# Stacked score operands laid out four partitions apart in a fused attention and convolution kernel

## The reference

```python
x = x + attention(group_norm(x))          # 32 groups
x = x + masked_conv3x3(group_norm(x))     # 256 -> 256 channels
# attention, its low half ("local scores" in this kernel): 4 heads of 32
q = (tokens @ l_q_w).reshape(B, H * W, 4, 32)             # 1024 tokens
kv = (pooled @ l_kv_w).reshape(B, 256, 2, 4, 32)          # 2x2 mean-pooled: 256 keys
attn = softmax(einsum('bnhd,bmhd->bhnm', q, k) * 32 ** -0.5)
lo = einsum('bhnm,bmhd->bnhd', attn, v) @ l_proj_w + l_proj_b
```

## Time and profile before

| | us |
|---|---|
| median of 3 runs | 351.7 |
| lowest, highest | 351.23, 353.86 |
| the profiled execution | 350.24 |
| its span in the profile | 348.0 |

### The profile page before, as it was taken

The page is one execution under the profiler, slowest core; times in us unless marked ns, Lnnn a source line. Parts: engine busy times, 40 slices in busy tenths (PEclk is TensorE's granted clock), DMA queues, the critical chain, the costliest instruction groups (busy, mean ns, idle before and its releaser), DMA issues.

```text
span 348.0 us, 4160 instructions
## 1 busy us (share of the span) xinstructions
PE 312.7 (90%) x1566; PEld 224.1 (64%) x1566; DVE 271.2 (78%) x489; ACT 148.7 (43%) x189; POOL 83.5 (24%) x46
## 2 busy tenths in 40 slices
PE   1996648999979899999799999999799999999995
PEld 1575334367866663788577745888488727877884
DVE  4953999679997696989979867789777847897572
ACT  2551628672582743553047854351255423031300
POOL 2026384540455020004900200008600200202000
PEclk9998958999989999999899999999899999999999
DMA  8789230009600000098011100296001000101002
GB/s 276 274 111 157 83 122 0 2 24 126 78 0 4 2 1 2 20 129 140 4 60 60 63 0 2 43 130 117 4 0 62 0 0 10 53 0 62 0 0 121
DMA packets 12067, 20.38 MB, mean 59 GB/s; under 512 B 2064, under 2 KB 8080, under 8 KB 11792
## 3 DMA queue, kind: packets, MB, share of 16 engines
q1 hardware_dynamic: 12048, 20.13, 28.3%
HBM read 7.93 MB, written 4.19 MB: 35 GB/s over the span
## 4 chain that ended last, share of the span: by engine, by line
PE 59%; DVE 26%; ACT 6%; issue 5%; DMA 3%; SPq 0%; DVEq 0%
PE slot L1136 29%; PE cps L1168 17%; DVE l_max L868 7%; PE slot L1212 7%; ACT probs L580 3%; PE cps L1212 2%; DMA ks<-probs 2%; DVE v_lo L834 1%; DVE mask L804 1%; PE cps L1136 1%; PE slot L1461 1%; DMA xy<-x 1%; DVE xy L909 1%; ACT p_w L628 1%; DVE xn L760 1%
## 5 line engine op out<-in xcount | busy, mean ns | idle before, releaser
L1168 PE MATMUL cps<-v_hi,cw_hi 128*128 128x512 f32 (+1 forms) x144 | 58.9, 409 | 3.6 <-DVE v_lo L834 2.9
L1168 PE MATMUL cps<-v_hi,cw_lo 128*128 128x512 f32 (+1 forms) x144 | 58.8, 409 | 0.0
L1168 PE MATMUL cps<-v_lo,cw_hi 128*128 128x512 f32 (+1 forms) x144 | 57.5, 399 | 0.0
L385 POOL TENSOR_TENSOR probs<-q_w,k_w 128x1024 f32<-128x1024 f32 x14 | 32.9, 2383 | 82.4 <-DVE rw L797 72.4
L868 DVE TENSOR_REDUCE l_max<-slot 128x4 f32<-128x1024 f32 x32 | 37.0, 1218 | 7.3 <-PE slot L1136 7.3
L580 ACT ACTIVATE probs<-slot 128x1024 f32<-128x1024 f32 x32 | 31.5, 1022 | 14.9 <-PE slot L1136 14.8
L1168 PEld LDWEIGHTS cps<-v_hi,cw_hi 128*128 128x128 f32 x144 | 28.1, 195 | 13.0 <-issue 5.3
L1168 PEld LDWEIGHTS cps<-v_hi,cw_lo 128*128 128x128 f32 x144 | 28.1, 195 | 7.7 <-issue 2.2
L1168 PEld LDWEIGHTS cps<-v_lo,cw_hi 128*128 128x128 f32 x144 | 28.1, 195 | 5.2
L368 POOL TENSOR_TENSOR mask<-rw 128x1024 f32<-128x1024 f32 x8 | 15.2, 1912 | 56.6 <-DVE rw L797 56.6
L1136 PE MATMUL slot<-xn_hi,w_hi 128*128 128x512 f32 (+1 forms) x68 | 27.2, 400 | 0.3 <-DVE xn_lo L726 0.3
(11 more groups left out here) (197 smaller groups left out, 633.5 us busy)
## 6 DMA issues: line engine op xcount, KB each, us to landing
xy<-x SPq DMA_DIRECT2D x8, 512.0 KB, 3.9
out<-xy SPq DMA_DIRECT2D x8, 512.0 KB, 2.6
qs<-probs SPq DMA_DIRECT2D x12, 256.0 KB, 5.8
qs<-probs SPq DMA_DIRECT2D x24, 128.0 KB, 8.2
raw_cw<-conv_w SPq DMA_DIRECT2D x2, 1152.0 KB, 6.8
ks<-probs SPq DMA_DIRECT2D x12, 128.0 KB, 6.9
probs<-h_qkv SPq DMA_DIRECT2D x2, 192.0 KB, 3.8
probs<-l_kv SPq DMA_DIRECT2D x2, 128.0 KB, 3.7
```

Source lines behind the costliest of these rows:

```text
L385: nc.gpsimd.tensor_tensor(product(b, j).rearrange("p (n w) -> p n w", n=NW), q_w[:].rearrange("p (n w) -> p n w", n=NW), k_w[:, j * G:(j + ...
L1168: ins = nc.tensor.matmul(cps[:, pos % 2, y0 * WT:y1 * WT], (cw_hi, cw_hi, cw_lo)[part][:, k, pos, dy + 1, o * P:(o + 1) * P], (v_hi, v_lo, ...
```

## The change

The three parts are no longer side by side. Part p of channel d goes to partition 4d + p, so each stacking DMA writes 32 partitions, four apart, over all 128. The fourth rows (4d + 3) take what stood in 96 and 97: the parts of the maxima go to partitions 3 and 7 (`SHIFT`). Both matmuls now contract over all 128 rows. For that, all of `ks` is set to 1.0 and all of `qs` to 0.0 by GpSimd at the start, where only two rows of `ks` were set. Since the block scores of the next image must not see the old maxima, SP zeroes partitions 3 and 7 of `qs` before each later image, with two DMAs of 16 KB from the zero columns of `l_max` (rows of 256 bytes), after a wait for all exponentials of the image before (`st_exp`); TensorE's wait on `stacked` counts them. For image 0, SP waits for the memsets (`ones`).

```diff
@@
-SC = 3 * HD
-SM = SC + 2
+PARTS = P // HD
+SHIFT = (PARTS - 1, 2 * PARTS - 1)
@@ stack(b), on SP
                 def queries(part, parts, n, done):
-                    sp.dma_start(qs[HD * part:HD * (part + 1), :, n].bitcast(F32),
+                    sp.dma_start(qs[bass.ds(part, HD, step=PARTS), :, n].bitcast(F32),
                                  parts[:, n].bitcast(F32)).then_inc(done, 16)
 
                 def keys(part, parts):
-                    sp.dma_start(ks[HD * part:HD * (part + 1)].bitcast(F32), parts.bitcast(F32)).then_inc(stacked, 16)
-
+                    sp.dma_start(ks[bass.ds(part, HD, step=PARTS)].bitcast(F32),
+                                 parts.bitcast(F32)).then_inc(stacked, 16)
+
+                if b == 0:
+                    sp.wait_ge(ones, 1)
+                else:
+                    sp.wait_ge(st_exp, b * LT)
+                    for i, row in enumerate(SHIFT):
+                        sp.dma_start(qs[row:row + 1].bitcast(F32),
+                                     l_max[i * 64:(i + 1) * 64, NB * HEADS:NB * HEADS + 64]).then_inc(stacked, 16)
                 sp.wait_ge(lq_act, b + 1)
@@ stack_maxima(b), on SP
-                    sp.dma_start(qs[SC + i:SC + i + 1].bitcast(F32), t.bitcast(F32)).then_inc(max_stacked, 16)
+                    sp.dma_start(qs[SHIFT[i]:SHIFT[i] + 1].bitcast(F32), t.bitcast(F32)).then_inc(max_stacked, 16)
@@
-        STACK, STACK_LATE, MAX_STACK = 6 * 16, 3 * 16, 2 * 16
+        STACK, SHIFTS, STACK_LATE, MAX_STACK = 6 * 16, 2 * 16, 3 * 16, 2 * 16
@@ GpSimd, at the start
-            nc.gpsimd.memset(ks[SC:SM].bitcast(F32), 1.0).then_inc(ones, 1)
+            nc.gpsimd.memset(qs[:].bitcast(F32), 0.0)
+            nc.gpsimd.memset(ks[:].bitcast(F32), 1.0).then_inc(ones, 1)
@@ pooled_scores(b, i), on TensorE
-                    last = mm(slot[score_slot(b, i)][:, half], ks[0:SM, h, t * P:(t + 1) * P], qs[0:SM, h, halves(half)],
+                    last = mm(slot[score_slot(b, i)][:, half], ks[:, h, t * P:(t + 1) * P], qs[:, h, halves(half)],
@@ block_scores(b, n), on TensorE
-                    ins = mm(flat[block_slot(b, n)][:, h * G:(h + 1) * G], qs[0:SC, h, n * P:(n + 1) * P], ks[0:SC, h],
+                    ins = mm(flat[block_slot(b, n)][:, h * G:(h + 1) * G], qs[:, h, n * P:(n + 1) * P], ks[:, h],
@@ front(b, conv), on TensorE
-                        pe.wait_ge(stacked, (b + 1) * STACK)
+                        pe.wait_ge(stacked, (b + 1) * STACK + b * SHIFTS)
```

## The result

| | before | after |
|---|---|---|
| median | 351.59 us (4 runs) | 345.87 us (4 runs) |
| lowest, highest | 351.23, 353.86 | 345.54, 346.5 |
| the profiled execution | 350.24 | 345.54 |
| its span | 348.0 | 343.7 |

The account below looks back on a forecast made before the run. Bound: image 0's scores wait for slow stacking copies, a bandwidth backlog at 126 GB/s. Maxima 4.6 us sooner, all else 0: 350.24 − 4.6 = 345.6 profiled, 351.7 − 4.6 = 347.1 us median; range 345.8 to 350.2.

Parts of the forecast that it names:

- Step 1: Image 0's stacking copies: rate rises from 126 towards 370 GB/s, first scores at about 26.0, 3.3 us sooner.
- Step 2: VectorE's maxima of image 0: without a standstill they end at 36.3 instead of 40.85, 4.6 us sooner.
- Step 3: After image 0's maxima: these end last, so the softmax and all later stages shift by about 4.5 us.
- Step 4: GpSimd's memsets at the start: end at 5.8 to 9.0 us, cost nothing; without slack 1.4 us at most.
- the first bound: GpSimd's memsets at the start: time goes by elements in a row, 4.8 us for 4096 + 1024, ending at 5.8.
- Step 5: SP before each later image: its wait and zeroing DMAs, some 1.2 us, are hidden in a gap of over 15.
- Step 6: TensorE's score matmuls: contraction over 128 rows instead of 96 or 98 costs nothing, 0.40 us either way.
- Step 7: Block scores and maxima of later images: gain of 0 to 0.3 us, taken as 0.
- A: Stacking copies speed up little: 351.7 us at 126 GB/s, 349 at 160; chance 0.08 unchanged, 0.09 partial.
- D: Stacking copies four rows apart crowd fewer write ports, 63 GB/s, time near 385 us; chance 0.04.
- C: At the start, the memset holds up VectorE's first statistics, a slip of 1.6 us, time 348.7; chance 0.04.
- B: In other phases, moved VectorE and GpSimd meetings and clock falls hand back 1 to 2 us, 348.5 to 350; chance 0.07.

Follow-up runs that it names:

- the first control: The changed kernel again, unaltered, run beside the trials of turn order and early x: 346.48 us, ratio 0.9864 to the kernel before.
- the second: The changed kernel once more, unaltered, run beside the kernel with both groups of GpSimd's convolution weights held back: 346.05 us, ratio 0.9865 to the kernel before.
- the first trials: Old rows in the changed kernel (349.55 us), value_half(1) earlier in the kernel before (349.4), maxima turned before window scores in the changed kernel (349.08); kernel before beside them 350.51.
- the second set: The changed kernel with further copies appended after its last store, varying source rows, size and which 32 rows are written: 385.63 us, one run.
- the first trial: The changed kernel with GpSimd's outer convolution weights held until VectorE finishes image 0's window softmax: 346.86 us, ratio 0.9879 to the kernel before.

## Why the prediction was right, point by point

**Bound.** Right: the wait at the earlier trace rows was one for bandwidth. With the old rows alone it comes back whole. The 1.2 us to the first byte and the 0.8 us of completion in that sum stand in none of its rows.

**Step 1, the rate.** Right in kind and size: between 126 and 370 the upper end was taken, and 381 came out. The landing was over-estimated, without effect. The estimate was 2.3 to 2.6 us, and the DMA issues of the changed kernel show 2.1:

```profile
ks<-probs SPq DMA_DIRECT2D x12, 128.0 KB, 2.1
```

TensorE did not wait for the keys at all. The scores start at 25.71 and not 26.0 because TensorE starts them 0.23 us behind the start of the last value matmul (25.48), where the forecast counted from its end at 25.88. The argument that the destination alone sets these copies apart was too simple, since an HBM source writes the same rows at 228.

**Step 2, the maxima.** The term was 4.6 us and measured 5.2. End forecast 36.3, seen 35.62. The 0.7 between them: 0.3 from the earlier start of the scores, 0.1 because VectorE follows TensorE after 0.75 us and not 0.85, 0.2 because no gap is left, and 0.1 because the eight take 9.16. The granted clock was 1.00 from 20 to 34 us, as the step needed.

**Step 3, what follows.** This step failed. "So VectorE's maxima end last" left out one order: TensorE turns the maxima only after the window scores, and these need GpSimd's last product. The prediction had that product's end right (35.0; seen 34.99) but set it only against ScalarE's need. That end was itself an effect of the change: before, GpSimd waited 2.90 us for the second half of the values and ended at 37.86. Four matmuls more and the turning may start at 36.9, where the maxima alone would have had it at 35.8, and with it come `group_means` and the window softmax. Before, the maxima ended last at 40.85 and GpSimd's products, at 37.86, had 3 us to spare; now the products and the window scores behind them are the later ones. Of the 5.2 us, 1.1 are handed back here. The two errors, 0.6 too little in step 2 and 1.1 too much here, leave 4.1 us. The span is 0.2 us shorter elsewhere, and the time outside the span 0.4 us shorter (350.24 − 348.0 = 2.2, 345.54 − 343.7 = 1.8), which no step has. That makes 4.7: forecast 345.6 for the profiled execution, seen 345.54. So closely the sum came out by luck; its terms were further off. ScalarE's statistics, forecast to start at 31.7 and end at 36.1, start at 32.50 and end at 36.96; the run with x early shows that this costs nothing.

**Step 4, memsets.** Free, and the first bound was the right one:

```profile
0.99 3.52 POOL L447 MEMSET qs<- 128x4096 f32 x1
4.45 0.95 POOL L448 MEMSET ks<- 128x1024 f32 x1
```

3.52 us where 3.8 was forecast, the end at 5.4, and the next work at 7.65 against 7.64 before; 2.25 us of slack are left. Time goes by elements in a row: 0.95 us for 1024 whether 2 partitions or 128.

**Step 5, SP.** Right. The zeroing DMAs are issued at 55.74 and the queries behind them at 72.28, so 16 us pass between. For images 2 and 3 it is 17 and 20 us.

**Step 6, 128 rows of contraction.** Right, though it is 32 or 30 more rows and not "two to four":

```profile
L1145 PE MATMUL slot<-qs,ks x64: 388/396/775, 40.8 to 272.2; 128*128 128x512 f32 x64
```

**Step 7, later images.** Right at 0, and the sign of being wrong that it had, image 1 waiting on its copies, did not show: its first scores wait 0.62 us for ScalarE and not for a DMA.

```profile
84.44 1.22 PE L1145 MATMUL slot<-ks,qs 128*128 128x256 f32 x8 [0.62 <-ACT v_w L524]
```

Image 1 is instructive. Its maxima's parts reach SP at 102.45 instead of 107.45, 5.0 us sooner, while the image as a whole starts 4.2 sooner. But the next thing on its chain is GpSimd's products, 9.42 us from 95.69, and TensorE's last window scores behind them at 105.16. The 0.8 us extra are gone by the next image (141.94 against 146.16).

**From the profiled execution to the median.** The forecast took the offset of 1.5 us to hold for the changed kernel too. It was 0.33 there, which is 1.1 of the 1.2 us between 347.1 and 345.87. The granted clock of the stretch from 26 to 62 us differs between executions of one kernel. In the windows of the profiled executions of the changed kernel it was 0.97 from 26 to 44 us and 0.84 from 44 to 62 in the first, 0.92 and 0.79 in the first control, 0.96 and 0.85 in the second, and the spans were 343.7, 344.7 and 343.3. The larger scatter of the kernel before goes with the clock too: of the 25 executions beside the first trials the slowest, 353.8 us, has the lowest mean granted clock, 0.951, and the five under 349.7 us have 0.970 to 0.974. Which of the two causes the other no run shows.

**The rivals.** A fell with 381 GB/s, D with the same number, C with the first statistics ending at 6.69 us in both kernels (4.10 + 2.59, 4.17 + 2.52 before). B named the right kind of outcome but the wrong mechanism: part of the gain was handed back, by TensorE's order. The meeting of VectorE and GpSimd that B was about is the same in both kernels (1.74 and 1.72 us for the cast). In the weighing of the rivals, a gain of 4 us would be 347.7 and not 347.9.

## What to carry to other kernels

When a copy inside SBUF is on the path, look at GB/s beside the DMA share: here a full share at a third of the rate of the loads came from the placement of the rows, and a layout in which the same number of rows is spread over all partitions gave the whole rate. After an early operand, walk the in-order queue of every engine that stands between it and the end, not only the engine that was late: what a gain meets next is often an instruction that merely stands ahead. And where a small instruction takes several times its usual duration, see which instruction of another engine ends with it, and move that one behind all that it can meet, not only behind the first.

## What the runs showed of the hardware that was not expected

- A copy from SBUF to 32 adjacent partitions moves 127 GB/s and the same from HBM 228; four apart they move 381 and 268 (the last at a DMA share of 0.87, so the engines were not full). Three apart from SBUF gives 247 and two apart 120. A source of 32 adjacent partitions is slow as well (186), with the destination on all 128. Why an HBM source is faster into adjacent rows than an SBUF source was not settled.
- Small bursts hardly show the limit. The first microsecond of the last group of the second set moved 236 GB/s to adjacent rows, and the rest 121 to 127. Four copies of 64 KB keep the engines busy for the same 0.9 us in sum with either placement (SP needs 0.6 us to issue each, and the engines run dry between them); four of 128 KB keep them busy for 2.9 us with adjacent rows and 1.6 us with rows four apart.
- 32 rows four apart (381) are as fast as all 128 rows (383).
- Two short VectorE instructions on 128 columns last until 0.1 us after a GpSimd instruction that reads SBUF: 1.72 and 1.79 us beside it, 0.23 and 0.29 without. GpSimd's own instructions stretch too when VectorE has the longer ones (1.85 to 2.70 us): in the first trial the VectorE instruction at 53.55 ends at 56.40, 1.1 us after GpSimd's (55.32), as if the two took turns. The Trainium skill, SBUF — State Buffer, section Who interferes with whom, says that VectorE's casts in a two-port mode, and VectorE instructions with two SBUF inputs, share a port pair with GpSimd, and that the one that issues first blocks the other fully. The rows agree in that both instructions end only after GpSimd's; whether the cast ran in a two-port mode no row shows.
- GpSimd memsets running until 5.40 us beside VectorE's first statistics delay them by nothing that counts (they start at 4.10 us and take 2.59, against 4.17 and 2.52 before).
